# Rotary attention stage: the context bank copied out by VectorE instead of ScalarE

## The reference

```
x = x + tanh(g_xattn[2]) * L2_xattn(layernorm(x), ctx)
x = x + tanh(g_ffn[2])   * L2_ffn(layernorm(x))

L2_xattn: q = rms_norm(x @ wq) (16 heads of 128), k = rms_norm(x @ wk) (4 key heads)
          k_ctx = rms_norm(ctx @ wk_ctx), v = x @ wv, v_ctx = ctx @ wv_ctx
          q, k = rotary(q), rotary(k)
          scores = q @ [k_ctx, k]^T / sqrt(128), causal over the second half
          out = softmax(scores) @ [v_ctx, v];  return out @ wo
L2_ffn:   gate, val, out: linear layers with rows rounded to 8 bits and
          ternary weights; out(silu(gate(x)) * val(x))
```

## Time and profile before

| | us |
|---|---|
| median of 3 runs | 2508.88 (2505.51 to 2517.94) |
| the profiled execution, its own time | 2485.77 |
| its span, first to last instruction | 2483.6 |
| PE busy | 2174.7 (88%) |
| VectorE busy | 1512.0 (61%) |
| ScalarE busy | 1125.3 (45%) |
| POOL busy | 745.6 (30%) |
| the stage in question, about | 1090 to 1927 of the span |

### The profile page before, as it was taken

The page is one execution under the profiler, slowest core; times in us unless marked ns, Lnnn a source line. Parts: engine busy times, 40 slices in busy tenths (PEclk is TensorE's granted clock), DMA queues, the critical chain, the costliest instruction groups (busy, mean ns, idle before and its releaser), DMA issues. The chain is left out here.

```text
span 2483.6 us, 38366 instructions
## 1 busy us (share of the span) xinstructions
PE 2174.7 (88%) x10438; PEld 1376.0 (55%) x10486; DVE 1512.0 (61%) x3702; ACT 1125.3 (45%) x3555; POOL 745.6 (30%) x932
## 2 busy tenths in 40 slices
PE   6969999988888688879999999999995788869999
PEld 3446677756455344435556656665653444445685
DVE  6975434456455577765676777677765577753244
ACT  2021244411455355545565556555552477742242
POOL 5705500056233200023344444344433100003104
PEclk9969999999999899999999999999997699979999
DMA  6902245453200000000000000000000000201143
GB/s 218 300 21 85 91 136 161 147 163 114 118 1 0 3 1 0 0 26 1 1 1 1 0 0 0 0 0 0 0 0 1 5 5 4 84 24 42 61 134 100
DMA packets 85587, 127.18 MB, mean 51 GB/s; under 512 B 12418, under 2 KB 74626, under 8 KB 84226
## 3 DMA queue, kind: packets, MB, share of 16 engines
q1 hardware_dynamic: 75490, 98.52, 12.5%
q0 software_dynamic: 9984, 27.28, 3.5%
HBM read 91.41 MB, written 47.84 MB: 56 GB/s over the span
## 5 line engine op out<-in xcount | busy, mean ns | idle before, releaser
L2371 ACT ACTIVATE l2x_prob<-l2x_pS,l2x_nb,l2x_rms_q 128x256 f32<-128x256 f32 x256 | 142.5, 565 | 116.5 <-DVE l2x_nb L2606 114.7
L1035 ACT ACTIVATE moe_act_g<-moe_pG 128x96 f32<-128x96 f32 (+1 forms) x159 | 53.2, 335 | 267.2 <-PE moe_pU L968 186.9
L1186 PE MATMUL l2x_pQ<-big,l2x_xT 128*128 128x512 f32 x312 | 149.6, 602 | 4.7 <-DVE l2x_part L2584 4.3
L2603 DVE TENSOR_REDUCE l2x_negmax<-l2x_pS 128x2 f32<-128x512 f32 x128 | 87.7, 685 | 92.5 <-PE l2x_pS L2191 89.7
L928 POOL DMA_INDIRECT moe_yk<-route_y,moe_slot_i x72 | 71.1, 987 | 218.9 <-DMA route_y<-moe_y 188.5
L3113 DVE TENSOR_TENSOR l3f_hid<-l3f_act_g,l3f_pA 128x256 f32<-128x256 f32 (+1 forms) x103 | 38.1, 370 | 159.0 <-ACT l3f_act_g L3024 117.6
L2201 PE MATMUL l2x_pOT<-l2x_probT,l2x_v 128*128 128x512 f32 x256 | 124.7, 610 | 4.5 <-ACT l2x_probT L2386 4.5
L2191 PE MATMUL l2x_pS<-l2x_kT,l2x_qT 128*128 128x256 f32 x512 | 128.3, 380 | 0.0
L2937 PE MATMUL l3f_pA<-big,l3f_xnT 128*128 128x512 f32 x256 | 125.4, 614 | 0.0
L2210 PE MATMUL l2x_pT<-big,l2x_oT 128*128 128x256 f32 x512 | 121.1, 379 | 0.7 <-ACT l2x_oT L2379 0.7
L1515 ACT ACTIVATE l1f_ex<-l1f_pS,l1f_negmax 128x128 f32<-128x128 f32 x256 | 73.0, 368 | 104.0 <-DVE l1f_negmax L1546 104.0
(11 more groups left out here) (498 smaller groups left out, 5753.1 us busy)
## 6 DMA issues: line engine op xcount, KB each, us to landing
route_x<-in_c_zero SPq DMA_DIRECT2D x1, 13184.0 KB, 81.6
moe_xg<-route_x SPq DMA_DIRECT2D x103, 128.0 KB, 2.2
route_y<-moe_y SPq DMA_DIRECT2D x103, 128.0 KB, 1.7
big<-in_e_gu SPq DMA_DIRECT2D x1, 6144.0 KB, 19.0
l3f_xg<-route_x SPq DMA_DIRECT2D x39, 128.0 KB, 2.2
route_y<-l3f_y SPq DMA_DIRECT2D x39, 128.0 KB, 1.7
big<-in_f_gu SPq DMA_DIRECT2D x1, 4096.0 KB, 12.2
big<-in_e_down SPq DMA_DIRECT2D x1, 3072.0 KB, 25.0
```

The source lines that it names most:

```text
L1186: last = pe.matmul(out, lhsT=xT[:, k, :], rhs=w[:, k, cols], start=(k == 0), stop=(k == KC - 1))
L2371: ins = act.activation(prob[g % 2][:, h, :], pS[j][:, (h % 2) * 2 * P:(h % 2 + 1) * 2 * P], ACT.Exp, scale=rms_q[g][:, h:h + 1], bias=nb[: ...
L2603: dve.tensor_reduce(negmax[:, c], pS[j][:].rearrange("p (h k) -> p h k", h=2), AX.X, ALU.max, negate=True).then_inc(S["max_steps"], 1)
```

## The change

The copy of pOT to oT is taken from ScalarE's order and put into VectorE's, as a `tensor_copy` with the same two waits and the same semaphore. In slots 0 to 2 it stands at the end of the slot, behind `f_second` and ahead of `nm.normalise` (slot 0) or `mul` (slots 1 and 2) of the next batch. In slot 3 it stands within `f_second`, between `f_hidden(b - 2, 1)` and `f_quant_h`; in the last batches' drain it stands between the last two `add_out`. The line numbers of the diff are those of the file.

```diff
--- before.py
+++ after.py
@@ -2373,11 +2373,6 @@
                                          accum_out=sums[g % 2][:, h:h + 1])
                 ins.then_inc(S["exp_done"], 1)
 
-            def values(b, p, g):
-                act.wait_ge(S["ot_ps"], 4 * b + g + 1)
-                after(act, S["out_ps"], 4 * b + g)
-                act.activation(oT[:].rearrange("p h t -> p (h t)"), pOT[:], ACT.Copy).then_inc(S["ot_read"], 1)
-
             def probs(b, p, g, j):
                 N = 4 * b + g
                 act.wait_ge(S["pT_ps"], 2 * N + j + 1)
@@ -2442,8 +2437,6 @@
                     evacuate(b + 1, 1 - p, g - 2)
                 if g < 2:
                     evacuate(b, p, g + 3)
-                if at_least(b, g, 1):
-                    values(*before(b, p, g, 1))
                 if g == 0:
                     value_rows(b, p, 0)
                 if not last:
@@ -2461,7 +2454,6 @@
             def finish():
                 probs(B - 1, 1, 3, 0)
                 probs(B - 1, 1, 3, 1)
-                values(B - 1, 1, 3)
                 for b in (B, B + 1):
                     for g in range(4):
                         f_middle(b, g)
@@ -2623,6 +2615,11 @@
                 dve.scalar_tensor_tensor(x, pT[:, C:2 * C], G["tg"][:, 2:3], x, ALU.mult,
                                          ALU.add).then_inc(S["added"], 1)
 
+            def values(b, p, g):
+                dve.wait_ge(S["ot_ps"], 4 * b + g + 1)
+                after(dve, S["out_ps"], 4 * b + g)
+                dve.tensor_copy(oT[:].rearrange("p h t -> p (h t)"), pOT[:]).then_inc(S["ot_read"], 1)
+
             def f_constants():
                 dve.wait_ge(F["const_in"], 48)
                 dve.tensor_scalar(f_val_b, f_val_b, 0.5, None, ALU.mult).then_inc(F["const_ready"], 1)
@@ -2714,8 +2711,13 @@
                         f_hidden(b - 2, 0)
                     if is_batch(b - 3):
                         f_add(b - 3, 1 - p)
+                if g < 3 and is_batch(b) and at_least(b, g, 1):
+                    values(*before(b, p, g, 1))
                 if g == 3 and is_batch(b - 2):
                     f_hidden(b - 2, 1)
+                if g == 3 and is_batch(b):
+                    values(b, p, 2)
+                if g == 3 and is_batch(b - 2):
                     f_quant_h(b - 2, p)
 
             def prepare0():
@@ -2755,6 +2757,7 @@
 
             def finish():
                 add_out(B - 1, 1, 2)
+                values(B - 1, 1, 3)
                 add_out(B - 1, 1, 3)
                 for b in (B, B + 1):
                     for g in range(4):
```

## The result

The changed kernel takes 2519.8 us in the median of 20 runs (2514.96 to 2527.92), the kernel before 2505.57 in 20 runs of its own on the same chip (2499.25 to 2517.94). The ratio is 1.0047, with a 95% interval of 1.0035 to 1.006: slower by 11.8 us, 8.8 to 15. (The two medians alone differ by 14.2 us, which lies inside that interval; the ratio is read here.) The forecast was 12 us more.

A forecast was written before the change was run, and what follows sets the result against it. PE was taken to bound the stage. Slot 3's 10.4, slot 0's 1.2 and the rest's 0.2 made 11.8, called 12 us, taking the median from 2508.9 to 2520.9 us; 8-in-10 range 2508 to 2530.

The forecast's parts named there:

- The bound and the path: PE bounds the stage; ScalarE or VectorE instructions count only if PE waits for them; relieving ScalarE is worth 0.
- Slot 3: Copy stands behind f_hidden's 1.58 us on VectorE; PE starts 0.80 us later in 13 batches: 10.4 us.
- Slot 0: Copy starts at PE's release but takes 0.083 us longer in 15 batches: 1.2 us; the delayed normalisation costs nothing.
- Slots 1 and 2: Copy fits VectorE's idle time and PE reads the rows only later: 0 for both.
- The sum: Slot 3's 10.4, slot 0's 1.2 and 0.2 for the rest: 11.8, called 12 us.
- Rival B: Slot 3: f_hidden runs in 0.68 us, out of the copy's way; 2.6 us in all, 2511.5; chance 0.15.
- Rival C: Slot 0: POOL's quantiser, starting later, blocks VectorE's nb product 1.58 us longer; 20.5 us more, 2541.4; chance 0.08.
- Rival D: Relieved ScalarE shortens PE's 16.7 and 5.5 us waits for it; half of 22.2 us gone, 2497.8; chance 0.10.

The follow-up runs named there:

- turn_early_vector: Changed kernel with PE's transposes of the normalised rows moved ahead of the value rows in slot 0; ratio to the kernel before 1.0077.
- hidden_first: Changed kernel with slot 3's f_hidden(b - 2, 1) moved ahead of add_out; ratio to the kernel before 1.0028.
- copy_first: Changed kernel with VectorE's copy in slot 3 moved ahead of f_hidden(b - 2, 1); ratio to the kernel before 1.0019.
- slot3_scalar: Changed kernel with slot 3's copy alone given back to ScalarE's old place; ratio to the kernel before 1.0032.
- copy_last: Changed kernel with slot 3's copy behind f_quant_h instead of ahead of it; ratio to the kernel before 1.028.
- scores_and_turned_vector: Last kernel tried: changed kernel, half of slot 1's scores (PE) and the turned hidden rows' eviction (ScalarE) moved earlier, within slot 0; ratio to before 0.9995.

## Why the prediction was right

- **The bound and the path.** That only what delays PE counts, held: the stage's length followed PE's waits, or its clock behind one (with the exception of slot 0 in the last kernel above, where the delay is there and no wait is put down), and the 35.7 us taken from ScalarE bought nothing.
- **Slot 3**, predicted 13 x 0.80 = 10.4 (0.70 to 0.92 each), measured 13 x 0.72 = 9.4. The chain is as forecast (f_hidden 1.58, copy 0.07 into it, copy 0.68). The term that was mis-sized is the hand-over to PE: I took 0.15 us from VectorE's last write, from the nearest bank of the earlier trace rows; it was 1421.33 - 1421.27 = 0.06, as quick as ScalarE's, the low end. In slot 0 it is 1433.56 - 1433.41 = 0.15, and ScalarE's there was 0.14: it goes with the place and not with the engine. f_quant_h came 0.49 us later and the quantiser 0.39, where 0.60 was forecast; with 3 us of slack it made no difference.
- **Slot 0**, predicted 15 x 0.083 = 1.2, measured 15 x 0.10 = 1.5: the copy took 0.691 us, where the other stage's row had 0.680. The normalisation behind the wait is covered, as turn_early_vector shows by taking the cover away. It even fell from 1.20 to 0.40 us, since it no longer runs beside POOL's addition; I had kept the 1.20 as a bound and had not said why it was long.
- **Slots 1 and 2**, predicted 0. True where a next product follows after idle time. In the last batch there is none: slot 2's copy sits late there, ahead of the maxima, and PE's next wait for ScalarE's probT is 2.35 us in place of 1.74. The step "I take 0 for both" left that one out. The wait after it fell from 1.11 to 0.78 us, so the drain grew by 0.27 in all, 22.03 to 22.30 us from slot 1's copy to the last.
- **The sum.** 9.3 (13 x 0.717, unrounded) + 1.5 + 0.2 (slot 3 of batches 0 and 1) + 0.3 (the drain) = 11.3, as measured for the stage; predicted 11.8, and 11.8 by the ratio. That the last two agree to the digit is luck: the interval is 8.8 to 15, and a slot 3 taken 1.1 us too high stands against terms taken 0.6 too low. So is part of the closeness of 2519.8 to the 2520.9 forecast, which was counted from a median of 2508.88 and not 2505.57. PE's waits came to 24.8 us over 28 times (27 forecast), of 0.88 and 0.97 (0.86 and 1.05 forecast); two of the 14 in slot 3 are of batches without f_hidden, 0.44 each, which the 27 overlooked.
- **Rival B** (f_hidden at 0.68) did not occur; hidden_first and copy_first show its price: 0.19 and 0.21 us more a batch and 5 us of stage, 2 of them in the drain, where B had said 2.6.
- **Rival C** (the quantiser blocks nb): nb took 0.16 us inside the quantiser here too, in all 26 cases. But the mechanism is not absent, as other rows show. In the kernel before, an nb at the start of slots 2 and 3 meets POOL's addition 30 times; it then takes 0.72 to 0.73 us and ends 0.02 behind the addition:

```profile
1424.60 1.26 POOL L2484 TENSOR_TENSOR l2x_rows<-l2x_part 128x512 f32<-128x512 f32 x1
1425.15 0.73 DVE L2606 TENSOR_TENSOR l2x_nb<-l2x_negmax,l2x_rms_q 128x2 f32<-128x2 f32 x1
```

In copy_first, where nb starts only 0.43 to 0.52 us behind the quantiser's start in 13 cases, it takes 0.53 to 0.62 and ends 1.05 behind that start every time:

```profile
1426.50 2.78 POOL L2487 TENSOR_SCALAR l2x_f_qh_q<-small 128x1024 bf16<-128x1024 f32 x1 [3.77 <-issue]
1427.02 0.53 DVE L2598 TENSOR_TENSOR l2x_nb<-l2x_negmax,l2x_rms_q 128x2 f32<-128x2 f32 x1
```

Every nb that starts 0.91 us or more behind it takes 0.16, in every kernel. The Trainium skill (SBUF — State Buffer, "SBUF: two separate sides") states an exclusive lock that is held for the whole instruction. In these traces that shows for the addition, but of the quantiser's 2.78 us only for about the first 0.9 (an estimate: 1.05 less nb's own 0.16; spans on POOL are rough). C did not occur because nb came later than that, and not because the quantiser can't hold VectorE back.
- **Rival D** (less waiting for ScalarE): 16.7 and 5.7 us, as before. No.

## What to carry to other kernels

When a short instruction moves to another engine, its own duration matters little (0.09 us here, 1.7 of the 11.3); what matters is what that engine's order puts ahead of it at the moment when its input is ready, so look there, slot by slot, for the latest releaser. A wait of the bounding engine on a bank's hand-over can be filled with independent work of its own, and each such move is to be followed by a look at what then waits on the engine behind. Compare a stage inside one execution, and not the spans of two.

## What the runs showed that I had not expected

**The clock after a short idle.** In the drain PE waits 2.35 us once. In the changed kernel its clock stayed full behind it, and in turn_early_vector too; in copy_first it didn't. The timeline and a window of the changed kernel, then of copy_first:

```profile
1908.61 0.63 PE L2220 MATMUL l2x_pP<-ident,l2x_prob 128*128 128x128 f32 x4 [2.35 <-ACT l2x_probT L2381]
1909.08 1.89 PE L2210 MATMUL l2x_pT<-big,l2x_oT 128*128 128x256 f32 x8
```
```profile
1909.00:1914.00 5.00, 4.22 (x20) 2.80 (x19) 3.14 (x7) 1.92 (x6) 0.00 (x0) 1.00 0.00 0
```
```profile
1905.11 0.65 PE L2220 MATMUL l2x_pP<-ident,l2x_prob 128*128 128x128 f32 x4 [2.35 <-ACT l2x_probT L2381]
1905.57 3.58 PE L2210 MATMUL l2x_pT<-big,l2x_oT 128*128 128x256 f32 x8
```
```profile
1905.00:1910.00 5.00, 4.89 (x15) 3.73 (x16) 1.59 (x6) 1.82 (x6) 0.00 (x0) 0.66 0.02 3
```

The same eight matmuls took 3.58 us instead of 1.89. hidden_first, slot3_scalar, copy_last and scores_and_turned_vector had the same, and its 1.7 us are most of the 1.9 to 2.2 us by which the stages of copy_first, slot3_scalar and hidden_first came out longer than expected. Why one idle of 2.35 us costs the clock and another doesn't, was not settled.

**Instruction fetches.** Taking one copy a batch out of ScalarE's loop raised the packets of an instruction queue from 56 to 82, and in one kernel's profile went with a stall of 1.3 us in every second batch; with instructions that do nothing useful in its place neither was there. For the packets that is cause and effect, for the stall it isn't shown.

**Who starts first.** An addition on POOL and a product of two SBUF tiles on VectorE don't share the delay: the one that started second was stretched, by 0.9 us on VectorE (0.68 to 1.58) or 0.39 on POOL (1.26 to 1.65). The small nb product was stretched by the addition too (0.16 to 0.73), and by the quantiser only near its start.
